# Attention's last product in 256-column halves, with the probabilities stored twice, in a one-core transformer block

## The reference

```
h = x @ mix[batch]                            # 64x64 mixing of the tokens, chosen by batch
q, k, v = h @ Wq.T, h @ Wk.T, h @ Wv.T        # 32 query heads, 8 key/value heads of 128
q, k = rmsnorm(q), rmsnorm(k)
p = softmax(q @ k.T / sqrt(128) + alibi, causal)   # within a batch: 64 x 64
x = x + (p @ v) @ Wo.T
x = x + ffn(lora_linear(x))                   # all linear: folded into one matrix at setup
```

## Time and profile before

| | |
|---|---|
| median of 3 runs | 2400.43 us (2400.09 to 2401.31) |
| the profiled execution | 2400.53 us, of which the span of the instructions is 2398.7 us |
| busy: PE, PEld, DVE, ACT, POOL | 99%, 82%, 73%, 55%, 12% of the span |
| granted TensorE clock, mean | 0.997 |
| chain that ended last | PE 94%, DVE 4%, issue 1%, DMA 1% |
| DMA | 316 MB, 132 GB/s on average |

### The profile page before, as it was taken

One profiled execution on the slowest core, in us unless ns is written; L12 is line 12 of the kernel. 1 busy time (PEld: TensorE's weight loads), 2 busy tenths in 40 slices (PEclk: granted clock), 3 DMA queues, 4 the chain that ended last, 5 costly groups with the idle time before them and its releaser, 6 DMA issues.

```text
span 2398.7 us, 32788 instructions
## 1 busy us (share of the span) xinstructions
PE 2368.9 (99%) x11578; PEld 1967.4 (82%) x11578; DVE 1750.3 (73%) x2866; ACT 1330.4 (55%) x3305; POOL 280.5 (12%) x336
## 2 busy tenths in 40 slices
PE   8989999999999999999999999999999999999998
PEld 6878888888888888888888888888888888888886
DVE  6768878686847867777856777777876686868682
ACT  4246656566625656566724656565744565657560
POOL 0222010101111001010011101010011101010110
PEclk9999999999999999999999999999999999999999
DMA  7765434441542242423343242423244242424250
GB/s 258 257 256 199 154 134 148 140 149 63 188 145 92 88 139 76 141 79 129 134 156 118 71 158 71 158 71 123 97 170 148 77 147 69 153 77 141 70 194 35
DMA packets 88436, 316.12 MB, mean 132 GB/s; under 512 B 12716, under 2 KB 13228, under 8 KB 87124
## 3 DMA queue, kind: packets, MB, share of 16 engines
q1 hardware_dynamic: 70292, 247.14, 30.5%
q0 software_dynamic: 16256, 62.92, 7.2%
q10 hardware_dynamic: 1728, 3.98, 0.5%
HBM read 282.54 MB, written 31.46 MB: 131 GB/s over the span
## 4 chain that ended last, share of the span: by engine, by line
PE 94%; DVE 4%; issue 1%; DMA 1%; ACT 0%; POOL 0%; ACTq 0%; POOLq 0%; DVEq 0%
PE main L1019 79%; PE pv_bank L1215 4%; PE qt_bank L1180 3%; PE s_bank L1196 2%; PE s_bank L1197 2%; PE pt_bank L1204 1%; PE pt_bank L1019 1%; DVE ring L1480 1%; DVE act_lo L1480 0%; DVE act_lo L1483 0%; DVE setup L1480 0%; PE qt_bank L1117 0%; PE s_bank L1117 0%; DMA mask<-in_masks 0%; DMA t_scratch<-sums 0%
## 5 line engine op out<-in xcount | busy, mean ns | idle before, releaser
L1019 PE MATMUL main<-ring,act_hi 128*128 128x512 f32 x3584 | 1149.2, 402 | 0.1
L1019 PEld LDWEIGHTS main<-ring,act_hi 128*128 128x128 f32 x3584 | 641.3, 189 | 112.7 <-issue 2.1
L1019 PE MATMUL main<-ring,act_lo 128*128 128x512 f32 x1792 | 702.5, 392 | 0.0
L1019 PE MATMUL main<-ring,lefts 128*128 128x512 f32 x2688 | 624.3, 391 | 0.0
L1480 DVE TENSOR_TENSOR ring<-raw,ring 128x1024 fp32r<-128x1024 f32 x448 | 554.4, 1240 | 59.5 <-ACT ring L1226 58.0
L1019 PEld LDWEIGHTS main<-ring,lefts 128*128 128x128 f32 x2688 | 501.7, 188 | 103.0
L1226 ACT ACTIVATE ring<-raw 128x1024 fp32r<-128x1024 f32 x448 | 472.5, 1057 | 180.8 <-PE main L1019 163.6
L1019 PEld LDWEIGHTS main<-ring,act_lo 128*128 128x128 f32 x1792 | 336.8, 188 | 74.6
L1816 POOL TENSOR_TENSOR rstd<-mean,half 128x4 f32<-128x4 f32 (+1 forms) x192 | 174.7, 910 | 1568.5 <-DVE mean L1605 1568.3
L1385 ACT ACTIVATE prob<-score,peak 128x64 f32<-128x64 f32 x512 | 136.7, 338 | 157.3 <-DVE peak L1660 156.8
L1357 ACT ACTIVATE sq<-main 128x128 f32<-128x128 f32 x640 | 168.8, 277 | 70.7 <-PE main L1019 68.4
(11 more groups left out here) (172 smaller groups left out, 2390.4 us busy)
## 6 DMA issues: line engine op xcount, KB each, us to landing
raw<-in_wq SPq DMA_DIRECT2D x128, 512.0 KB, 4.0
raw<-t_scratch SPq DMA_DIRECT2D x128, 512.0 KB, 3.3
raw<-in_wo SPq DMA_DIRECT2D x96, 512.0 KB, 3.3
raw<-in_wkv SPq DMA_DIRECT2D x64, 512.0 KB, 4.1
sums<-in_wo POOLq DMA_DIRECT2D x32, 512.0 KB, 6.6
t_scratch<-sums POOLq DMA_DIRECT2D x32, 512.0 KB, 4.2
raw<-f_scratch SPq DMA_DIRECT2D x32, 512.0 KB, 5.5
acc<-in_x POOLq DMA_DIRECT2D x16, 512.0 KB, 3.7
```

Of the source, the lines that this page charges most:

```text
L1019: mm = eng.matmul(bank, a, b, start=start and n == 0 and m == 0, stop=stop and n == len(terms) - 1 and m == 2, skip_group_check=further)
```

## The change

1. `values` takes the place of `v_hi` and `v_lo`: [128, tiles, 2 heads, 2 batches, 128]. For batch b the partitions of batch b hold the hi part of its values, and the other 64 partitions hold the lo part of the same values. `v_hi` becomes two copies of 64 partitions, `v_lo` two subtractions of 64 partitions that write the other half, and it waits for `v_hi`.
2. A new stage `p_twice` (ScalarE, 8.3) copies each batch's `pt_hi` into the 64 partitions that were zero. It stands in the list behind `p_hi` (8), behind the `square` (8.15) of step k+2, and ahead of `p_lo` (8.6).
3. `pv` is, for each batch, `values` by `pt_hi` and `values` by `pt_lo`: four matmuls of 256 columns. The first gives hi by hi and lo by hi in one contraction. It waits for `p_twice`.
4. `pv` moves from 10 to 10.6 and `heads` from 10.7 to 11.5, which is a quarter later each. For the last q step of a block the additions in `LATE` shrink from 2.1 to 1.6.

```diff
-          tp=7.9, tp_hi=8, tp_lo=8.6,
-          v=10, v_hi=10.7, v_lo=11.3,
+          tp=7.9, tp_hi=8, tp_again=8.3, tp_lo=8.6,
+          v=10.6, v_hi=11.5,
...
             self.at(base, when("tp_hi"), lambda: self.add("p_hi", k))
+            self.at(base, when("tp_again"), lambda: self.add("p_twice", k))
...
-        v_hi = sb("v_hi", [P, TILES, 2, HD], F32R)
-        v_lo = sb("v_lo", [P, TILES, 2, HD], F32R)
+        values = sb("values", [P, TILES, 2, BPT, HD], F32R)
...
-                    for m, (a, p) in enumerate(((v_hi, pt_hi), (v_hi, pt_lo), (v_lo, pt_hi))):
-                        mm = eng.matmul(pv_bank[:, :, :].rearrange("p b n -> p (b n)"), a[:, t, g % 2, :],
-                                        p[:, :, :].rearrange("p b n -> p (b n)"), start=m == 0, stop=m == 2)
+                    for b in range(BPT):
+                        both = values[:, t, g % 2, b, :]
+                        eng.matmul(pv_bank[:, b, :], both, pt_hi[:, b, :], start=True, stop=False)
+                        mm = eng.matmul(pv_bank[:, b, :], both, pt_lo[:, b, :], start=False, stop=True)
...
+                    for b in range(BPT):
+                        act = eng.activation(values[rows_of(b), tile_of(k), :, b, :], values_in(k, b), ACT.Copy)
+                    act.then_inc(done["v_hi"], 1)
...
+                elif stage == "p_twice":
+                    k, = key
+                    w.wait_ge("p_hi", k)
+                    for b in range(BPT):
+                        act = eng.activation(pt_hi[rows_of(1 - b), b, :], f32(pt_hi[rows_of(b), b, :]), ACT.Copy)
+                    act.then_inc(done["p_twice"], 1)
...
+                    w.wait_ge("v_hi", k)
+                    for b in range(BPT):
+                        rest = eng.tensor_tensor(values[rows_of(1 - b), tile_of(k), :, b, :], values_in(k, b),
+                                                 f32(values[rows_of(b), tile_of(k), :, b, :]), ALU.subtract)
+                    rest.then_inc(done[stage], 1)
```

More of the change, by code:

```diff
@@ L51 @@
           w_hi=0.3, w_lo=0.9)
-LATE = dict(s=0.5, s_add=0.5, s_exp=0.5, s_norm=0.5, tp=1.1, tp_hi=1.1, tp_lo=1.1, v=2.1, v_hi=2.1)
+LATE = dict(s=0.5, s_add=0.5, s_exp=0.5, s_norm=0.5, tp=1.1, tp_hi=1.1, tp_again=1.1, tp_lo=1.1, v=1.6, v_hi=1.6)
 OPS = (("11", "11", "a"), ("s3", "t3", "d"), ("12", "21", "a"), ("s2", "t2", "b"),
@@ L799, in build_program @@
         bias_parts = k_flat.rearrange("p (u s n) -> p u s n", u=2, s=2)
-        enc_rows = [v_hi[:, :, :, :].rearrange("p a b n -> p (a b n)"), v_lo[:, :, :, :].rearrange("p a b n -> p (a b n)")]
-        enc_hi = v_hi[0:ENC, :, :, :].rearrange("p a b n -> p (a b n)")
-        enc_lo = v_lo[0:ENC, :, :, :].rearrange("p a b n -> p (a b n)")
+        v_flat = values[:, :, :, :, :].rearrange("p t g b n -> p (t g b n)")
+        enc_rows = [v_flat[:, 0:CHUNK], v_flat[:, CHUNK:2 * CHUNK]]
+        enc_hi, enc_lo = (part[0:ENC, :] for part in enc_rows)
         x_even = [lefts[:, 2, i, :, :, :].rearrange("p a h n -> p (a h n)") for i in range(2)]
@@ L907, in norm_bank, with values_in @@
             return bank_of("mm", k, 0)
+        def values_in(k, b):
+            return norm_bank(k)[rows_of(b), 2 * HD:4 * HD].rearrange("p (j n) -> p j n", j=2)
         def norm_width(k):
@@ L1208, in _ @@
                     kind, blk, g, t = step(k)
-                    w.wait_ge("p_hi", k)
+                    w.wait_ge("p_twice", k)
                     w.wait_ge("p_lo", k)
@@ L1349, in _ @@
                         w.wait_ge("weff_mm", KT, 1, 3)
-                    copy(v_hi[:, tile_of(k), :, :], norm_bank(k)[:, 2 * HD:4 * HD].rearrange("p (j n) -> p j n", j=2), "v_hi")
+                    for b in range(BPT):
+                        act = eng.activation(values[rows_of(b), tile_of(k), :, b, :], values_in(k, b), ACT.Copy)
+                    act.then_inc(done["v_hi"], 1)
                 elif stage == "square":
@@ L1608, in _ @@
                     w.wait_ge("square", k)
-                    low(v_lo[:, tile_of(k), :, :], norm_bank(k)[:, 2 * HD:4 * HD].rearrange("p (j n) -> p j n", j=2),
-                        v_hi[:, tile_of(k), :, :], stage, k)
+                    w.wait_ge("v_hi", k)
[3 more added lines that the diff above has]
+                    rest.then_inc(done[stage], 1)
                 elif stage == "scale":
```

## The result

| | before | after |
|---|---|---|
| median (lowest to highest), 6 runs each, side by side | 2400.02 us (2399.28 to 2401.31) | 2415.81 us (2413.90 to 2417.94) |
| profiled execution, span | 2400.53, 2398.7 us | 2414.47, 2412.7 us |
| chain that ended last: PE, DVE, ACT | 94%, 4%, under 1% | 71%, 16%, 8% |

The ratio is 1.0066, with an interval from 1.0055 to 1.0077. The change makes the kernel slower by 15.8 us, where I had forecast 2398.0 and a range up to 2406. The granted TensorE clock is not the cause: its mean is 0.997 in both profiled executions, and both have it at 0.5, the lower level of 1.2 GHz, in the same three short stretches (from 155.5, 660.7 and 2391.2 us before, and from 156.8, 662.0 and 2406.2 us after).

A forecast was written before the change was run, and what follows sets the result against it. TensorE, busy 62.88 of 63.00 us, was taken as the bound. Saving 25.8 us less 22.9 given back left 2.9, less 0.5 for late steps: 2400.53 to 2398.1, or 2398.0 as median; range 2385 to 2406.

The forecast's parts named there:

- the saving: TensorE's `pv`: four matmuls of 256 columns replace three of 512, saving 0.20 us in each of 128 steps, 25.8 us.
- both mechanisms: `p_twice` delays `scale` and 28 `query_t` loads; halved values delay `gain` and `key_t` loads in three of four kv steps.
- the added work: Busy time added: 101 us on ScalarE for `p_twice` and 24 for `v_hi`, 27 us on VectorE for `v_lo`.
- term 1: Last step of a q unit: `p_twice` delays `w_hi`, `w_lo`, `scale` and the `query_t` load, losing 7.6 us.
- term 2: Last step of a kv unit: halved `v_hi` delays `key_t` by 0.51, `v_lo`'s second half hidden; 8.2 us lost.
- if `prob_t` waits: Sign of a wrong prediction: TensorE's `prob_t` transposes waiting; the sum gave no loss there.
- The second kv step: Second step of 12 kv units: `v_lo` delays `scale` by 0.11 and `pv`'s 0.20 is waited away; 3.7 us lost.
- (a): Rival: the 64-partition halves overlap on ScalarE, so only 12.3 us is given back; 2387 us, chance 0.20.
- (b): Rival: late loads were mistaken for lost time, so nearly all the saving is kept; 2375 us, chance 0.08.
- (c): Rival: a `p_twice` pair above 1.0 us on ScalarE makes `exp`, `prob` and `prob_t` late; 2412 us, chance 0.14.
- (d): Rival: no change in TensorE's cost, 256 columns at the rate of 512; 2452 us, chance 0.03.

The follow-up runs named there:

- whole_v_lo: Changed kernel with VectorE's `v_lo` pair as one operation of 128 partitions, ScalarE's two copies kept, low values misplaced: 2407.94 us, ratio 1.0031.
- whole_values: Changed kernel with `v_hi` and `v_lo` each as one operation of 128 partitions, values misplaced: 2398.97 us, ratio 0.9996 to before.
- no_p_twice: Changed kernel without the second copy of the probabilities, leaving out the products of low values with probabilities: 2399.28 us, ratio 0.9997 to before.
- offsets_only: Kernel before with only the later offsets of `pv` and `heads`: 2401.70 us, ratio 1.0006.
- p_twice_gpsimd: Changed kernel with the second copy of the probabilities on GpSimd instead of ScalarE: 2400.99 us, ratio 1.0002 to before.
- both_gpsimd: Changed kernel with second copy on GpSimd, values split by whole operations and placed by three GpSimd copies, full result: 2387.26 us, ratio 0.9944 to before.
- both_gpsimd_later: The GpSimd kernel with both rearrangements, its three placing copies also waiting for `gain`: 2426.41 us, ratio 1.0115 to before.

## Why the prediction was wrong

**Right: the saving.** 0.20 us for each `pv`, 25.8 in all, and the steps of q units with nothing else in them show it. So are both mechanisms, their places and their counts: 28 steps forecast to wait for `scale` (28 of the 29 waits, two of which were there before), the loads waiting for `gain` in three of four kv steps and over 30 us (32.7). So is the added work: 106.6 us for `p_twice` (101), 48.5 for `v_hi` (24 more), 54.0 for `v_lo` (27 more). The line of `p_twice` (busy us, mean ns of one):

```profile
L1409 ACT ACTIVATE pt_hi<-pt_hi 64x256 fp32r<-64x256 f32 x256 | 106.6, 416 | 4.6
```

**Wrong by size, term 1: "Lost: 0.27 x 28 = 7.6 us".** It was 0.49 a step, 13.5 in all. I had priced the pair at 0.79, from `p_hi`. It takes 0.87 (483.98 to 484.85), since each half takes 0.416 and not 0.378, and it starts 0.24 behind the last accumulator read where `w_hi` starts 0.10 behind it. Read from `p_hi` to `w_hi` it is 1.03 more than before, and 1.03 - 0.79 = 0.24 is about the difference, as the free slack had been used up already. The working itself has a slip that goes the other way: it sets 0.17 us of lateness as free, where the earlier trace rows give 0.23, so that by its own rows the term was 0.22 x 28 = 6.2.

**Wrong by size, term 2: "the second half of `v_lo` fits in the 0.46 us of idle time".** It didn't: 0.78 a step, not 0.51, 11.8 us and not 8.2. A second half of 0.42 to 0.44, a `v_lo` that starts 0.13 later behind `mean` (386.83 - 386.63 = 0.20, where whole_v_lo has 0.07), and a `w_lo` that starts only when the pair has ended, together take the 0.46 and 0.14 more; another 0.12 is lost between `w_lo` and `scale` (1.26 us, and 1.14 in whole_values). whole_v_lo splits the 0.78 into 0.52 for ScalarE and 0.26 for VectorE. This is the step that a reader could have caught: a cover of 0.46 for a need of 0.44 isn't a cover.

**Left out: `prob_t`.** My sum has nothing for the ends of the blocks. There the second copies make VectorE's list late as well. Behind the last q step of block 3 `prob` ends 10.96 us after that step's transposes, and 10.15 in no_p_twice; in both kernels VectorE goes without idle time of more than 0.04 us for 10 us before it, so nothing takes the lateness up. PE waits 0.56 us there for `prob_t`'s input, 2.3 us in four blocks, and 0 in no_p_twice. `exp` itself waits there for `peak` in both kernels (2.04 us before 1739.09 in the changed one), so ScalarE's queue isn't what holds it; where on the way from `p_twice` VectorE's list first falls behind wasn't traced. I had named this as a sign of being wrong ("if `prob_t` waits").

**Smaller ones.** The second kv step lost 0.46 and not 0.31, of which 0.09 is the later `pv` (offsets_only), a move I had costed at nothing. The first units of blocks 2 to 4 lost 3.6 besides their last steps, for which I had nothing; no_p_twice gives back 2.3 of it in their first steps. In sum the terms were too small by 5.9, 3.6, 1.8 and 0.6 (the four first lines of the table), 3.6 and 0.5: 16.0 us.

**The rivals.** (a) is out: no pair overlaps. (b) is out: PE's own waits for `gain` and `scale` went from 5.8 to 30.0 us. (c) named the price from which it turns, 1.0 us on ScalarE, and 1.03 was measured; but the size of it came from elsewhere. `exp` did become late in many steps (it waited for `peak` 120 times before, 156.8 us, and 68 times after, 96.2 us), and in most steps nothing followed from that: in no_p_twice, where it waits 124 times, the q steps other than the last have the same lengths as in the changed kernel. At the four block ends `prob_t` did wait, as (c) has it, but with an `exp` that was held by `peak` and not by ScalarE's queue. At 2412 (c) came nearest all the same. (d) is out by the timeline of `pv`.

Of the 15.8 us I had foreseen no part; my terms gave back 23.4 and the chip took 39.4. All of the errors have one sign: seams of 0.1 us, a cover that was too small and places taken for free, in chains without slack. My range assumed that they would err both ways.

## What to carry to other kernels

When TensorE is full, a saving on it is worth only what the chains that feed it can follow, so first look which loads wait for which engine, and price added work where it stands in those chains, with every seam between instructions. In this kernel an operation of 64 partitions took as long as one of 128 (0.38 and 0.39 us on ScalarE, 0.42 and 0.42 on VectorE): splitting one in two for the sake of a layout doubles it. A rearrangement that the chain doesn't wait for belongs on an engine that is idle (here GpSimd, 12% busy), but it has to be kept from long SBUF-to-SBUF operations of VectorE, and nothing that TensorE waits for may wait for its end.

## What the runs showed of the hardware

- *GpSimd and VectorE slow each other.* A GpSimd cast of 64x256 from SBUF takes 0.39 to 0.40 us with no such operation of VectorE beside it (p_twice_gpsimd), and up to 1.02 (both_gpsimd's lines above) or 1.46 us (p_twice_gpsimd) beside VectorE's two-input operations in SBUF. Those take up to 0.20 us longer (0.43 to 0.63, 1.22 to 1.42), while `scale`, with an input in PSUM, takes no longer. The Trainium skill (SBUF — State Buffer, SBUF: two separate sides) has this as an exclusive lock on a shared pair of ports: a VectorE operation with both inputs in SBUF and a GpSimd operation that reads SBUF don't share it, the one that comes later is blocked. The trace agrees in which operations are hit. That they are lengthened by 0.20 us and not by the other's whole length is what the rows show beside it.
- *Pairs of 64-partition operations on ScalarE don't overlap*, neither with each other nor with what comes ahead or behind: `values` 385.17, 0.78 for two, squares at 385.97; `p_twice` starts 0.02 after the end of the accumulator read ahead of it (483.74 + 0.22, 483.98). A copy of 128 partitions lets the squares start after 0.28 (384.30 and 384.58 in both_gpsimd). The cause of it isn't shown.
- *A copy from SBUF into other partitions* (`p_twice`) takes 0.416 us, 0.04 more than one from PSUM (0.378).
- *The granted clock can fall behind a wait of TensorE*: in both_gpsimd_later to 0.5 for 3.4 us, eight times, at 1.6 us each, after TensorE had been busy 1.73 of 4 us (831.80 to 835.80). After the waits of the changed kernel's last kv steps, about 0.7 us each, it stayed at 1.0.
